# Two folded steps, one slot order for all engines, and one filler at each place, in a two-stream transformer kernel

## The reference, cut to what matters

```python
x = x + ga * _L0_attn_ref(h, ...)   # sparse: 64 local keys and, by an index score, the best 32 others (top_k, gather)
x = x + gb * _L0_ffn_ref(h, ...)    # two layers of windowed attention and a GELU-gated MLP
x = x + ga * _L1_attn_ref(h, ...)   # 16 heads of size 8
x = x + gb * _L1_ffn_ref(h, ...)    # 16 experts of which 8 count, and a shared one
# in a layer of _L0_ffn_ref:
h = shift_token(x)
h = (h - mu) / jnp.sqrt(var + 1e-05) * lg + lb
h = h @ w1 + b1
a, g = jnp.split(h, 2, axis=-1)
h = a * jax.nn.gelu(g, approximate=False)
x = x + h @ w2 + b2
```

## Time and profile before

| | us |
|---|---|
| runs | 1538.6, 1540.81, 1547.84 (median 1540.81) |
| the profiled execution | 1539.22, its span 1537.4 |
| TensorE busy, of the span | 1346.2 (88%) |
| VectorE busy | 903.6 (59%) |
| ScalarE busy | 862.0 (56%) |
| GpSimd busy | 361.0 (23%) |

### The profile page before, as it was taken

One profiled execution on the slowest core, in us unless ns is written; L12 is line 12 of the kernel. 1 busy time (PEld: TensorE's weight loads), 2 busy tenths in 40 slices (PEclk: granted clock), 3 DMA queues, 4 the chain that ended last, 5 costly groups with the idle time before them and its releaser, 6 DMA issues. The chain is left out here.

```text
span 1537.4 us, 30694 instructions
## 1 busy us (share of the span) xinstructions
PE 1346.2 (88%) x11816; PEld 963.9 (63%) x11816; DVE 903.6 (59%) x2934; ACT 862.0 (56%) x2231; POOL 361.0 (23%) x580
## 2 busy tenths in 40 slices
PE   6789989898898998888898899988899899888797
PEld 5456657566665666665676566666676566556576
DVE  3855575745565756565366566556456655666634
ACT  3444666554544657555565375754665536665483
POOL 0422040211332222210153124030024320402002
PEclk9999999999999999999999999999999899999999
DMA  8121000000112100000011200000001210000000
GB/s 274 51 64 28 7 1 1 1 4 1 49 29 58 21 5 1 1 1 5 8 46 29 61 17 1 1 1 1 4 8 44 73 28 9 1 1 1 1 1 8
DMA packets 45618, 36.46 MB, mean 24 GB/s; under 512 B 32992, under 2 KB 37536, under 8 KB 44960
## 3 DMA queue, kind: packets, MB, share of 16 engines
q1 hardware_dynamic: 45472, 34.50, 7.9%
HBM read 25.46 MB, written 7.44 MB: 21 GB/s over the span
## 5 line engine op out<-in xcount | busy, mean ns | idle before, releaser
L1114 ACT ACTIVATE arena<-ps 128x512 f32<-128x512 f32 (+7 forms) x560 | 252.7, 482 | 229.9 <-PE ps L688 33.9
L550 PE MATMUL ps<-mean_mat 128*128 128x256 bf16 x2038 | 297.9, 279 | 5.7 <-DVE arena L1484 3.2
L550 PEld LDWEIGHTS ps<-mean_mat 128*128 128x128 bf16 x2038 | 189.7, 99 | 94.4 <-issue 56.5
L1892 POOL TENSOR_TENSOR arena<-arena 128x512 f32<-128x512 f32 x64 | 81.3, 1272 | 460.9 <-DVE arena L1497 460.4
L1320 ACT ACTIVATE arena<-arena,small 128x192 f32<-128x192 f32 (+1 forms) x256 | 129.8, 510 | 34.4 <-DVE small L1669 34.0
L1717 DVE TENSOR_REDUCE small<-ps 128x4 f32<-128x1024 f32 x64 | 75.3, 1219 | 24.2 <-PE ps L986 23.9
L1607 DVE TENSOR_TENSOR gath<-ps,rank_tab 96x512 f32<-96x512 f32 x96 | 63.3, 684 | 42.9 <-PE ps L578 42.6
L1770 DVE TENSOR_TENSOR arena<-arena,ps 128x512 f32<-128x512 f32 x64 | 42.9, 687 | 73.1 <-ACT arena L1414 57.9
L1477 DVE CUSTOM_DVE_ANT_0 arena<-ps,mask_w_bf 128x192 f32<-128x192 f32 (+1 forms) x256 | 67.4, 319 | 21.4 <-PE ps L664 21.3
L1268 ACT ACTIVATE arena<-arena,small 128x224 f32<-128x224 f32 (+1 forms) x128 | 56.6, 444 | 40.7 <-DVE small L1626 40.6
L757 PE MATMUL ps<-w_experts,arena 128*128 128x128 f32 x544 | 69.8, 280 | 10.3 <-DVE arena L1770 6.8
(11 more groups left out here) (279 smaller groups left out, 2915.5 us busy)
## 6 DMA issues: line engine op xcount, KB each, us to landing
idxb<-idx_scratch SPq DMA_DIRECT2D x24, 512.0 KB, 5.1
score_scratch<-arena SPq DMA_DIRECT2D x96, 64.0 KB, 1.7
w_experts<-in_experts SPq DMA_DIRECT2D x3, 1088.0 KB, 16.5
w_wqkv<-in_wqkv SPq DMA_DIRECT2D x1, 1536.0 KB, 9.7
arena<-score_scratch SPq DMA_DIRECT2D x96, 16.0 KB, 2.1
arena<-arena SPq DMA_DIRECT2D x96, 16.0 KB, 1.8
arena<-in_x SPq DMA_DIRECT2D x8, 128.0 KB, 2.2
out_x<-arena SPq DMA_DIRECT2D x8, 128.0 KB, 1.9
```

The source lines that it names most:

```text
L550: mm(to, still[:, 0:P], still, start=True, stop=True)
L1114: return act.activation(dst, src, ACT.Copy)
L1892: ins = pool.tensor_tensor(own, own, turned, ALU.add)
```

## The change

1. In the norms of the layers (N2, N3) the factor stays, and the shift ln_b goes into the bias: once, ahead of slot Q0.0 of the first round, layer_biases computes w1 times ln_b for both layers in 12 matmuls of one column, and VectorE adds it to b1 (b1_set). The product with rstd and the factor are then one instruction.
2. The projection of keys writes tokens 128 to 191 twice, into both halves of the partitions (a third block of kvsrc). In G5 and G6 the six matmuls of the second source take 64 rows each, the even bank's from the lower half, the odd bank's from the upper half, and alternate. Both banks of such a pair are complete at its end.
3. TURNS goes. slot_order walks the slots of both streams by estimated lengths, always the stream that is less far by their sum, stream 1 45 units behind, and one list serves all five engines.
4. BUSY becomes 1 at each place: 576 matmuls instead of 2038.

```diff
-    c["source"] = (np.arange(P)[:, None] + np.array([[0, P]])).astype(f)
+    c["source"] = np.stack([np.arange(P), P + np.arange(P) % LW], 1).astype(f)
-TURNS = {
...
+SLOTS = ([("F0", 1.2), ("N0a", 1.2), ("N0b", 2.0), ("F1", 3.5), ("F2", 2.2), ("F3", 2.5), ("F4", 2.8), ("F5", 2.8),
...
+            ("N5a", 1.2), ("N5b", 2.0), ("E0", 4.0), ("E1", 5.5), ("E2", 6.5), ("E3", 6.5), ("E4", 6.5), ("E5", 3.5),
+            ("E6", 2.0)])
+LAG = 45.0
+def slot_order():
+    where = [0.0, LAG]
+    left = [[(name, us) for r in range(ROUNDS) for name, us in SLOTS] for s in range(NS)]
+    gathered = 0
+    order = []
+    while any(left):
+        ready = [s for s in range(NS) if left[s]]
+        can = []
+        for s in ready:
+            name = left[s][0][0]
+            turn = gathered % NS == s
+            if name == "F9" and not turn:
+                continue
+            can.append(s)
+        s = min(can, key=lambda i: where[i])
+        name, us = left[s].pop(0)
+        if name == "G7":
+            gathered += 1
+            where[1 - s] = where[1 - s] if left[1 - s] and left[1 - s][0][0] != "F9" else max(where[1 - s], where[s])
+        where[s] += us
+        order.append((s, name))
     return order
+BUSY = ["1" * 400] * NS
...
-                    terms = [(m.kv_part[i][:, 0, :], hot[n][:, part]) for i in range(3)]
-                    if n == 2:
-                        terms += [(m.kv_part[i][:, 1, :], hot[3][:, part]) for i in range(3)]
-                    for i, (l_, r_) in enumerate(terms):
-                        last = mm(bank[g % 2][0:GF, :], l_, r_, start=(i == 0), stop=(i == len(terms) - 1))
-                    last.then_inc(*one("gather_mm"))
+                    for i in range(3):
+                        last = mm(bank[g % 2][0:GF, :], m.kv_part[i][:, 0, :], hot[n][:, part], start=(i == 0), stop=(n < 2 and i == 2))
+                    if n < 2:
+                        last.then_inc(*one("gather_mm"))
+                if n == 2:
+                    for i in range(3):
+                        for g in (2 * p, 2 * p + 1):
+                            part = slice(512 * (g % 4), 512 * (g % 4) + 512)
+                            rows_ = slice(64 * (g % 2), 64 * (g % 2) + 64)
+                            last = mm(bank[g % 2][0:GF, :], m.kv_part[i][rows_, 1, :], hot[3][rows_, part], start=False, stop=(i == 2))
+                            if i == 2:
+                                last.then_inc(*one("gather_mm"))
+            def layer_biases():
+                for l in range(2):
+                    for i in range(2):
+                        for c in range(3):
+                            n, c0, to = HC[c], HID * i + P * c, 6 * l + 3 * i + c
+                            last = mm(bank[3][0:n, to:to + 1], w1[:, l, c0:c0 + n], ln_gb[:, l, 1:2], start=True, stop=True)
+                last.then_inc(sig("b1_mm"), 1)
-                dve.tensor_copy(m.ckv_b, bank[2][:, 128:160])
+                dve.tensor_copy(m.ckv_b, bank[2][:, 192:224])
-                        dve.wait_ge(*at("gather_mm", g + 1))
+                        dve.wait_ge(*at("gather_mm", g + 1 if p < 4 else 2 * p + 2))
-                    ln_scaled(2 + l, m.hT, ln_gb[:, l, 0:1], ln_gb[:, l, 1:2])
+                    dve.wait_ge(*at("ln_rstd", 3 + l))
+                    dve.scalar_tensor_tensor(m.hT, bank[1][:, 0:L], ln_gb[:, l, 0:1], m.rstd, ALU.mult, ALU.mult)\
+                       .then_inc(*one("ln_out"))
```

More of the change, by code:

```diff
@@ L463, in sync_stream @@
                 of.r = r
-                for name in SLOTS:
+                for name, _ in SLOTS:
                     if name == "F8":
@@ L894, in tensor_stream @@
                     yield f"Q0.{l}"
+                    if (r, s, l) == (0, 0, 0):
+                        pe.wait_ge(sig("b1_set"), 2)
                     values(l, 1)
@@ L1330, in scalar_stream @@
                     yield f"N{2 + l}b"
+                    if r == 0 and l == 0:
+                        act.wait_ge(sig("b1_set"), 2)
                     table(act, ACT.Gelu)
```

96 lines of the change are left out of this document (37 added, 59 removed), and 6 rows, old and new, of the table SLOTS.

## The result

The changed kernel takes 1726.65 us (median of 4 runs, 1723.85 to 1727.87) against 1540.45 us: 1.120 times the time of before, 95% interval 1.1165 to 1.1235. The forecast was slower, 1629 us, at most 1710: the side was right, the size was not, 186 us instead of 89.

The account below looks back on a forecast made before the run. The prediction took two chains of dependent hand-offs (streams 0 and 1), sharing five in-order engines, to bound the kernel. Its sum, table loads the second -2: 1539.2 - 4 + 2 - 2 + 10 + 60 - 2 + 26 = 1629 us, range 1555 to 1710.

Parts of the forecast that it names:

- Folds (-4, +2): Layer norms: shift folded into bias saves 7.2 us of VectorE, -4 us of time; the one-time bias passes cost +2 us.
- Halves (-2): Gather's second source in half-array matmuls: up to 11 us of TensorE go, hand-off no shorter; -2 us, bounds -11 and +11.
- Fillers and clock (+10): TensorE: 1462 fewer fillers give -20 us, a clock falling from 0.98 to 0.90 costs +30 us; together +10 us.
- Orders (+60): One list replaces five tables, exposing hand-off waits on the engines: +60 us, bounds +10 and +150.
- (a): Stream 0's experts with stream 1's second attention: successive score pieces make TensorE wait, 9.6 us a round, 38 us in four.
- (b): Front's second query transpose: only one expert piece covers its 10.8 us hand-off; TensorE stands 5.1 us, 15 us in three rounds.
- (c): Small places, such as lost gather matmuls between A5 and A6 and norm halves back to back: two us a round, 8 us.
- Part is given back: half, 30 us: Of 61 us named order losses, half, 30 us, returns because the other stream is further on afterwards.
- The one list for ScalarE and VectorE (+30): ScalarE and VectorE: 136 more stream changes, one in seven exposing a 1.75 us hand-off, 34 us, taken as 30.
- Lag (+26): Stream 1 starts 33 us later and 25 us more stand alone at the end: +26 us, bounds 0 and 29.
- The low clock: Rival, chance 0.15: new stalls and missing fillers add up, clock 0.80 throughout, up to 1706 us.
- the order is neutral: Rival, chance 0.09: slack of 489 us swallows all but 10 us of the order's cost, lag costs 0; 1553 us.

Follow-up runs that it names:

- e3: Changed kernel with the five orders and 2038 fillers of before, so both folds (shift into bias, second source in halves) alone: 1540.4 us, 1.0002.
- e1: Kernel before, its five orders kept, with one filler at each place (576 instead of 2038): 1557.6 us, 1.0134.
- e2: Kernel before with the changed kernel's single list for all engines, its lag included, and all 2038 fillers kept: 1738.1 us, 1.1283.
- e9: Changed kernel with neighbouring entries of its one list exchanged, chosen by an offline replay; folds and one filler at each place kept: 1565.0 us, 1.0158.
- e14: Kernel of e9, the changed kernel's order put back where stream 0 is in its experts or the next round's first slots: 1622.1 us.
- e16: Kernel of e9, the changed kernel's order put back where stream 0 is in its two layers: 1612.8 us.
- e13: Kernel of e9, the changed kernel's order put back where stream 0 is in its second attention: 1598.5 us.
- e15: Kernel of e9, the changed kernel's order put back where stream 0 is in front (from F6), gather or first attention: 1607.8 us.
- e7: Changed kernel with planned lengths of slots E1 to E4 set to 3.0, so one score piece stands between expert pieces again: 1720.5 us, 1.1166.
- e4: Kernel before with TensorE's own list used on all five engines, 2038 fillers kept: 1600.7 us, 1.0399.
- e10: Kernel before with 2038 fillers and one list for all engines, found by the same replay from TensorE's own table: 1542.3 us, 1.0016.
- e5: Changed kernel with the lag of stream 1 set to 30 units instead of 45: 1790.1 us, 1.1609.
- e6: Changed kernel with the lag of stream 1 set to 60 units instead of 45: 1825.0 us, 1.1853.

## Why the prediction was right and wrong

**Folds (-4, +2): right.** VectorE 8.3 us less busy, the time unmoved.

**Halves (-2): right.** TensorE gained 7.1 us and the hand-off stayed as the working said: in the first such pair, from the first matmul to the end of the second eviction, 3.5 us before (71.75 to 75.27) and 3.7 in e3 (72.03 to 75.73). VectorE's eviction waited 42.9 us for the gather before and 45.5 in e3, and the kernel took the same time.

**Fillers and clock (+10): near in sum with the old orders, wrong inside.** e1 shows +18 (13 to 28 by its interval); with the planner's list the same step, and the folds with it, is -12 (e2 to after). The price of a filler, 297.9 / 2038 = 0.146 us, is a mean in which most stand in rows; alone one takes 0.295. So "TensorE busy near 1130 to 1200" was wrong at once, 1333 us. The clock was forecast 0.90 and came out 0.93 in e1 and 0.88 in after. My 61 us of added TensorE time are 54 in e1 and 109 in after; 44 of these are gone in e9.

**Orders (+60): here it failed.** e2 measures orders and lag together at 198 us, where the prediction had 86. Taken by its own parts:
- *The two places were seen rightly.* (a): "waits over 2 us, 8 times and more" behind the reduce: in the experts' stretches there are eight of 2.7 us, two a round; the other twelve of the 20 lie beside the layers. (b): in each of the three rounds 10.9 us lie between the end of the first query transpose and the second (forecast 10.8), with one expert piece in them. But the wait is split: 2.48 us before the ups, for ScalarE, and 2.68, 1.19 and 1.15 us before the transpose, for GpSimd; in the fourth round the ups between them run at a granted clock of 0.53 and last 3.50 us. That L735's waits add up to 17.4 us, near the forecast's 15, is luck: 12.4 of them lie in the first round, where stream 0 is alone:

```profile
46.94 1.11 PE L735 MATMUL ps<-packed,arena 128*128 128x128 f32 x4 [3.35 <-POOL arena L1913]
...
60.46 1.11 PE L735 MATMUL ps<-packed,arena 128*128 128x128 f32 x4 [9.01 <-POOL arena L1913]
...
1301.86 3.50 PE L754 MATMUL ps<-arena,w_experts 128*128 128x256 f32 x8 [2.48 <-ACT arena L1424]
...
1306.62 0.65 PE L735 MATMUL ps<-packed,arena 128*128 128x128 f32 x4 [1.15 <-POOL arena L1913]
```

- *Their price* was 44 us for three rounds (3 x 9.6 + 15); e14, which puts both back in three rounds, costs 57. The projection X0 behind its norm, in the same stretch and not named, waits 12.8 us there. "An expert round lasts 45 us" came true (47) with that help.
- *The list of places was taken for the whole.* (c), "small ones of the same kind, two us a round", 8 us, stood for everything else. e16 measures the layers at 48 us. The second attention has 16 us in e13's first three sequences, and in e15 23 of 37 us come after the first sequence. Of the waits, the one that comes and goes with its part most clearly is projection beside projection, 27 us of TensorE's. The prediction never looked there, since it had read the order at two places only; GpSimd, busy 23% of the span, was no suspect, but there both streams ask it at once.
- *"Part is given back: half, 30 us."* That step had no row under it, and the runs show the opposite: the parts add up (181 for 162). In e7, where one place was mended alone, some 14 us a round left the stretch and 6 us in all left the kernel, because the pieces taken out must stand somewhere; where a stall was added, nothing of it was given back.
- *The one list for ScalarE and VectorE (+30)*: by the count of changes. e4 shows 61 for giving up the five tables with TensorE's entries, so the size was half, and e9 and e10 show that the count was no measure: 551 and 567 changes, and no cost that can be told from that of five lists.

**Lag (+26): not measured alone, but bounded.** Stream 1 starts at 77.79 us (forecast 69.5), and 47.6 us at the end stand alone (forecast 48):

```profile
1675.38 0.73 POOL L2018 TENSOR_TENSOR arena<-arena 128x256 f32<-128x256 f32 x1
1722.97 0.72 POOL L2018 TENSOR_TENSOR arena<-arena 128x256 f32<-128x256 f32 x1
```

The list of e9 starts stream 1 at 35.20 us and has 26 us alone at the end, so it undid the lag as well, and its price is inside the 162 us. The later start is part of the 14 us that e15 has lost when the first sequence ends. The longer end is part of the 21 us that e13 loses in its last sequence. An estimate: a round of experts cost 17 us in e14, some 5 of it for the query transpose, which the last round lacks, and a second attention 5; that leaves some 4 us for the end. So the lag cost at most 35 us, by the estimate 18, and the orders 163 or more of e2's 198. e5 and e6 changed the lag and every meeting with it.

**The rivals.** The low clock (0.15, 1706 us) came nearest in time, but not as it was told: the clock is 0.88, not 0.80, and TensorE's idle time is the larger part of the loss, 202 us against 109. The recorded test said it: over 1710 us, either a clock under 0.85, or waits of VectorE on TensorE grown by over 100 us, "then orders". They grew by 152 (339 to 491). That the order is neutral, since 489 us of slack swallow it, fell: in e2, with the same fillers, idle time grew by 124 us, useful work by 56 and the fillers by 20, all of it on top of the span. Slack at one place took up nothing of the waits at another.

## What to carry to other kernels

When in-order engines share two chains of short hand-offs, a change of order is priced over all of its meetings: take every kind of meeting in a round, not the two that look worst, and don't discount the sum. Inside a stretch, follow every hand-off (norm to projection too), and keep what is lost at the start and end, where one chain is alone, apart from the rest. Look for the places where both chains ask the same little-used engine at once. And test a mended place by the length of the whole round: the stretch alone tells nothing.

## What the runs showed of the hardware

- A 256-column filler costs more alone than in a row: 0.295 us of TensorE's recorded busy time where each stands alone (e1), 0.146 us on average over the 2038 of before. One alone at the upper clock level shows 0.27 to 0.28 us, six in a row 0.82 (before, 1093.20), and one alone at the lower level 0.39 (after, 1218.85).
- The clock goes with the waits: with the same matmuls and fillers it was 0.97 with one list (e10) and 0.92 with another (e2), and useful work then took 1049 and 1105 us.
- Half-array matmuls (64 rows) that alternate between the halves took 0.142 us each against 0.231 for 128 rows, 0.6 of the time where full overlap would be 0.5.
